# Step two of a graph layer: the first pair's order, and who makes the lists of tied values

## The reference

```python
for n in range(2):                                  # the steps
    logits = (Xa @ W1.T @ W2.T) @ (Xa @ W3.T).T     # 3327 x 3327
    probs = softmax(logits)
    # nucleus: of each row the largest values are kept, until those
    # ahead of a value sum to 0.9; the order among equals is argsort's
    sp = take_along_axis(probs, argsort(-probs)); cs = cumsum(sp)
    mask = (cs - sp < 0.9) put back in place
    A = probs * mask / sum(probs * mask)
    Xf = R @ Xf                                     # R: adj + I, rows normed
    Xa = A @ Xa
    Z = Z + Xf @ U1[n].T + Xa @ U2[n].T
x = layernorm(X + Z)
```

## Time and profile before

| | us |
|---|---|
| median of three runs | 2841.34 |
| the profiled execution, by its own time | 2843.26 |
| span of the profiled execution | 2841.4 |
| TensorE (PE) busy | 2368.2 (83%) |
| VectorE busy | 2228.3 (78%) |
| ScalarE busy | 1071.9 (38%) |
| GpSimd busy | 97.5 (3%) |

### The profile page before, as it was taken

The page is one execution under the profiler, slowest core; times in us unless marked ns, Lnnn a source line. Parts: engine busy times, 40 slices in busy tenths (PEclk is TensorE's granted clock), DMA queues, the critical chain, the costliest instruction groups (busy, mean ns, idle before and its releaser), DMA issues. The chain is left out here.

```text
span 2841.4 us, 53527 instructions
## 1 busy us (share of the span) xinstructions
PE 2368.2 (83%) x17759; PEld 1995.4 (70%) x17759; DVE 2228.3 (78%) x6754; ACT 1071.9 (38%) x1785; POOL 97.5 (3%) x236
## 2 busy tenths in 40 slices
PE   5898998755888888887887728996999999999985
PEld 1566666444777676666676627895899999999952
DVE  3777778358887889887888967784999999999946
ACT  4566666422333334333343131002443434434323
POOL 0000000100000000000000010000000000000000
PEclk9999999977889998999998967998999999999997
DMA  3000000020222221222221232563233434343320
GB/s 125 2 1 1 1 1 2 1 73 25 98 98 98 97 98 50 98 83 75 77 107 50 97 126 100 214 216 124 98 130 116 137 107 145 103 144 109 112 86 25
DMA packets 57109, 245.02 MB, mean 86 GB/s; under 512 B 6705, under 2 KB 18352, under 8 KB 43120
## 3 DMA queue, kind: packets, MB, share of 16 engines
q1 hardware_dynamic: 56816, 241.94, 24.2%
HBM read 235.10 MB, written 6.82 MB: 85 GB/s over the span
## 5 line engine op out<-in xcount | busy, mean ns | idle before, releaser
L1906 PE MATMUL a_acc<-H,pT 128*128 128x128 f32 x4056 | 548.0, 277 | 11.3 <-ACT a_rows L1938 3.7
L1906 PEld LDWEIGHTS a_acc<-H,pT 128*128 128x128 f32 x4056 | 495.4, 192 | 28.3 <-DVE pT L2040 19.8
L913 PE MATMUL small<-XR,wT 128*128 128x128 f32 x2756 | 376.4, 282 | 30.4 <-ACT wT L1109 29.6
L71 DVE MAX8 cand<-e 128x8 f32<-128x64 f32 (+3 forms) x1898 | 302.5, 239 | 123.4 <-issue 123.4
L797 PE MATMUL lg<-kT,qs 128*128 128x512 f32 (+1 forms) x742 | 351.9, 614 | 46.0 <-ACT e L1053 36.1
L913 PEld LDWEIGHTS small<-XR,wT 128*128 128x128 f32 x2756 | 342.1, 196 | 46.6 <-ACT wT L1109 46.6
L2040 DVE TENSOR_TENSOR pT<-a_tr,a_adjT 128x512 f32<-128x512 f32 (+1 forms) x546 | 316.6, 645 | 22.6 <-PE a_tr L1865 19.2
L817 PE MATMUL accR<-XR,adj 128*128 128x129 f32 x2704 | 329.4, 284 | 0.0
L817 PEld LDWEIGHTS accR<-XR,adj 128*128 128x128 f32 x2704 | 326.3, 202 | 0.0
L1865 PE MATMUL a_tr<-ident,prob 128*128 128x128 f32 x2028 | 311.7, 274 | 10.9 <-ACTq L1932 10.9
L1109 ACT ACTIVATE wT<-tr 128x512 f32<-128x512 f32 (+1 forms) x371 | 206.1, 566 | 278.6 <-PE tr L903 276.7
(11 more groups left out here) (329 smaller groups left out, 2457.4 us busy)
## 6 DMA issues: line engine op xcount, KB each, us to landing
adj<-in_adjT SPq DMA_DIRECT2D x52, 1664.0 KB, 7.2
g_adj<-in_adjT SPq DMA_DIRECT2D x26, 1664.0 KB, 6.9
a_adj<-in_adj SPq DMA_DIRECT2D x26, 1664.0 KB, 6.9
a_adjT<-in_adjT SPq DMA_DIRECT2D x156, 256.0 KB, 3.9
a_adjT<-in_adjT SPq DMA_DIRECT2D x26, 128.0 KB, 4.2
XT<-in_x_t SPq DMA_DIRECT2D x1, 1664.0 KB, 13.4
hT_scratch<-hT SPq DMA_DIRECT2D x1, 1664.0 KB, 12.4
nsT_scratch<-nsT SPq DMA_DIRECT2D x1, 1664.0 KB, 6.2
```

Source lines behind the costliest of these rows:

```text
L71: eng.max(cand[:, n, :], src[:, n * seg:min((n + 1) * seg, width)])
L913: mm = eng.matmul(accA[:, :], wT[(k * NC + c - 1) % 2][:, o:o + P], xa[:, j, 0:P], start=(j == 0), stop=(j == T - 1))
L1906: mm = eng.matmul(acc[:, :], pT[g % RING][:, (j % 4) * P:(j % 4 + 1) * P], H[:, j, :], start=(j == 0), stop=(j == T - 1))
```

## The change

In step two alone:

1. GpSimd makes the grid ahead of the queries of pairs 0 and 1. TensorE makes its part of the grid after the logits of pair 0, ahead of those of pair 1. ScalarE copies the grid ahead of pair 0's exponentials, and copies unit 1's rows ahead of pair 1's exponentials.
2. A new function `find_marks` on GpSimd makes the drops and hits of both tiles of a pair, into buffers that now have room for two tiles. It waits for the pair's flags and for the selections of the pair before, and is done one pair ahead, between the scaling and the adding of rows. VectorE waits for the new semaphore `marks_ready` ahead of its selections and finds nothing more itself, but for the last batch. The instruction that moves `left` on is a function of its own, `pass_ties`, which runs only where more than 24 ties are to be marked.
3. In the first hop GpSimd scales the rows of both units of a pair before it adds either.

```diff
@@ Search
-        self.hits, self.drops = sb("hits", [P, TIES]), sb("drops", [P, 8])
+        self.hits, self.drops = sb("hits", [P, 2, TIES]), sb("drops", [P, 2, 8])
...
     def find_ties(self, eng, k):
+        hits = self.hits[:, k, :]
+        eng.tensor_scalar(hits, self.index[:, :], self.one("cut", k), None, ALU.mult)
+        eng.drain()
+        eng.tensor_scalar(hits, hits, self.one("left", k), self.one("cut_kept", k), ALU.is_lt, ALU.mult)
+        eng.drain()
+
+    def pass_ties(self, eng, k):
         eng.scalar_tensor_tensor(self.one("left", k), self.one("cut", k), -float(TIES), self.one("left", k),
                                  ALU.mult, ALU.add)
+        eng.drain()
...
-    def select(self, eng, k, e_pad, kind, flag, regs, both_ways):
+    def select(self, eng, k, e_pad, kind, flag, regs, both_ways, found=False):
...
         def divide():
-            if both_ways:
-                self.find_drops(eng, k)
-            self.find_ties(eng, k)
-            self.mark_ties(eng, 0, e_pad)
+            if not found:
+                if both_ways:
+                    self.find_drops(eng, k)
+                self.find_ties(eng, k)
+            self.mark_ties(eng, k, 0, e_pad)
...
@@ gpsimd
+                    def find_marks(p):
+                        eng.wait_ge(flags_ready, turn_of(step, p) + 1)
+                        eng.wait_ge(w_ready, seq(step, p, 0))
+                        eng.tensor_tensor(pool_gate[:, :], find.one("cut", 0), find.one("cut", 1), ALU.add)
+                        for k in range(2):
+                            find.find_drops(eng, k)
+                            find.find_ties(eng, k)
+                        eng.drain()
+                        eng.sem_inc(marks_ready, 1)
...
                         else:
+                            if hop == 0:
+                                for u, s in units_of(p, hop):
+                                    scale_rows(u, s)
+                            find_marks(p + 1)
                             for u, s in units_of(p, hop):
-                                if hop == 0:
-                                    scale_rows(u, s)
                                 add_rows(u, hop)
                             give_attended(p)
...
+                    if step == 1:
+                        make_grid()
                     for p in range(2):
                         give_q(p, 0)
                         give_q(p, 1)
-                    if step == 1:
-                        make_grid()
                     if step == 0:
                         over_pairs(eng, pair, tail=3)
                     else:
+                        find_marks(0)
                         over_pairs_with_rows(eng, pair_with_rows)
@@ tensor
                     for p in range(2):
                         logits(p, 0)
                         logits(p, 1)
+                        if step == 1 and p == 0:
+                            make_grid()
...
-                        make_grid()
                         for u, s in units_of(0, 0):
                             rows(u, 0)
@@ scalar
                     for k in range(2):
                         copy_logits(0, 0, k)
+                    if step == 1:
+                        copy_grid()
                     for k in range(2):
                         exps(0, 0, k)
...
-                        copy_grid()
                         copy_rows(0, 0, 0)
+                        copy_rows(1, 1, 0)
                         exps_of(1, 1)
-                        copy_rows(1, 1, 0)
@@ vector
-                        find.select(eng, k, e[b][k][:, :], kinds[k], flag, regs, step == 1)
+                        find.select(eng, k, e[b][k][:, :], kinds[k], flag, regs, step == 1,
+                                    found=step == 1 and not at(p, PAIRS))
...
                         assign_slots(p)
+                        eng.wait_ge(marks_ready, p + 1)
+                        eng.memset(gate[:, :], 0.0)
                         select(p, b, 0)
                         select(p, b, 1)
```

More of the change, by code:

```diff
@@ L416, in find_ties, with mark_ties, drop_ties @@
     def find_ties(self, eng, k):
-        eng.tensor_scalar(self.hits[:, :], self.index[:, :], self.one("cut", k), None, ALU.mult)
+        hits = self.hits[:, k, :]
+        eng.tensor_scalar(hits, self.index[:, :], self.one("cut", k), None, ALU.mult)
         eng.drain()
-        eng.tensor_scalar(self.hits[:, :], self.hits[:, :], self.one("left", k), self.one("cut_kept", k),
-                          ALU.is_lt, ALU.mult)
+        eng.tensor_scalar(hits, hits, self.one("left", k), self.one("cut_kept", k), ALU.is_lt, ALU.mult)
         eng.drain()
+    def pass_ties(self, eng, k):
         eng.scalar_tensor_tensor(self.one("left", k), self.one("cut", k), -float(TIES), self.one("left", k),
                                  ALU.mult, ALU.add)
+        eng.drain()
     def find_drops(self, eng, k):
-        eng.tensor_scalar(self.drops[:, :], self.index[:, 0:8], self.one("cut", k), None, ALU.mult)
+        drops = self.drops[:, k, :]
+        eng.tensor_scalar(drops, self.index[:, 0:8], self.one("cut", k), None, ALU.mult)
         eng.drain()
[L430 to L435, removed]
+        eng.tensor_scalar(drops, drops, self.one("over", k), self.one("cut_dropped", k), ALU.is_le, ALU.mult)
+    def mark_ties(self, eng, k, n, src):
+        eng.match_replace(out=self.work[:, :], in_to_replace=self.hits[:, k, 8 * n:8 * n + 8], in_values=src,
                           imm_value=BIG_E)
-    def drop_ties(self, eng):
-        eng.match_replace(out=self.work[:, ::-1], in_to_replace=self.drops[:, :], in_values=self.work[:, ::-1],
+    def drop_ties(self, eng, k):
+        eng.match_replace(out=self.work[:, ::-1], in_to_replace=self.drops[:, k, :], in_values=self.work[:, ::-1],
                           imm_value=-1.0)
@@ L459, in more_ties @@
             for n in range(TIES // 8):
-                self.mark_ties(eng, n, self.work[:, :])
+                self.mark_ties(eng, k, n, self.work[:, :])
                 eng.drain()
+            self.pass_ties(eng, k)
             eng.tensor_scalar(self.one("r_up", k), self.one("left", k), 0.0, 4.0, ALU.is_gt, ALU.mult)
@@ L481, in divide @@
                 self.find_ties(eng, k)
-                self.mark_ties(eng, 0, e_pad)
+                self.mark_ties(eng, k, 0, e_pad)
             eng.drain()
             if both_ways:
-                self.drop_ties(eng)
+                self.drop_ties(eng, k)
             with eng.If(eng.snap(flag) > 1):
                 eng.drain()
-                self.mark_ties(eng, 1, self.work[:, :])
+                self.mark_ties(eng, k, 1, self.work[:, :])
                 with eng.If(eng.snap(flag) > 2):
                     eng.drain()
-                    self.mark_ties(eng, 2, self.work[:, :])
+                    self.mark_ties(eng, k, 2, self.work[:, :])
                     eng.drain()
+                    self.pass_ties(eng, k)
                     while_over(eng, flag, 3, self.width // TIES, more_ties)
@@ L547, in layer0 @@
         qs = [sb(f"qs{i}", [P, P]) for i in range(2)]
-        gate = sb("gate", [P, 1])
+        gate, pool_gate = sb("gate", [P, 1]), sb("pool_gate", [P, 1])
         inv_sums = sb("inv_sums", [P, T])
@@ L589, in layer0 @@
         grid_ready, grid_made, grid_copied = sem("l0_grid_ready"), sem("l0_grid_made"), sem("l0_grid_copied")
+        marks_ready = sem("l0_marks_ready")
         slots_ready, taken_ready = sem("l0_slots_ready"), sem("l0_taken_ready")
```

## The result

The changed kernel took 2792.97 us, the median of four runs from 2790.32 to 2795.52, beside 2840.43 for the kernel before (four runs). The ratio is 0.9826 with a 95% interval of 0.9804 to 0.9848, so 49.4 us less (43 to 56). The profiled execution took 2795.35 us, with a span of 2793.6, TensorE busy 2358.4 (84%), VectorE 2201.9 (79%), ScalarE 1071.5 (38%), GpSimd 140.9 (5%).

What follows compares the result with a forecast made beforehand. VectorE's chain was taken to bound step two: 23.9 (first pair) + 33.6 (lists) - 1.0 - 1.2 = 55.3 us off the profiled 2843.26 gives 2788.0, median 2786.0. Range 2770 to 2806.

Steps and rivals of the forecast that it cites:

- VectorE is the chain in step two, and waits for other engines at two places only: Step two: time off VectorE comes off the span; it waits only for the grid, 19.0 us, and TensorE's flags, 16.1.
- Part one, 23.9: Start of step two: grid and unit one's rows copied earlier bring VectorE's first slot instruction to 618.6, gaining 23.9 us.
- The shift by 2.2: Start of step two: GpSimd's grid ahead of the first queries makes all up to the search come 2.2 us later.
- Part two, 33.6 for 13 pairs: Selections: drops and hits leave VectorE, 33.0 + 1.5 us, less 0.9 for a wait and memset per pair: 33.6 us.
- The lists are hidden: GpSimd's lists take about 4 us per pair under 19.9 us of cover; the last pair may lose 0 to 2.
- Scaling in the search, 1.0 lost: VectorE's search, six pairs: the second unit's scaling beside it costs 0.2 us each, 1.0 us in all.
- The lock rule: VectorE's search: shared port charges it GpSimd's 1.28 us in six pairs, 7.7 us, sum 48.6; rival at 2793, chance 0.05.
- TensorE's slack, 1.2 lost: TensorE's wait for flags at pair 12: its own way is 211.3 us, VectorE's would be 210.1, so 1.2 us is lost.
- all slack: TensorE's 15.0 us of waits for GpSimd's scaling go away, but all of it is slack today.
- the gaps stay: VectorE's 25 gaps ending in "issue", 63.5 us: the number of jumps stays; a change over 16 us refutes the prediction.
- the first rival: VectorE's gaps are dealt anew by the changed code, 16 us either way: 2770 or 2802; chance 0.12 better, 0.12 worse.
- the second, TensorE as the limit: In the pairs TensorE becomes the limit and half of the lists' gain is eaten: 2803 us; chance 0.08.

Runs made afterwards that it cites:

- e10: The changed kernel itself, unchanged, measured and profiled again: 2790.36 us, ratio 0.982.
- e1: The kernel before with only the first pair's new order (grid early, unit one's rows copied ahead of pair one's exponentials): 2816.33 us, ratio 0.9906.
- e2: The changed kernel with the old order at the start of step two, so only the lists on GpSimd: 2809.52 us, ratio 0.9888.
- e4: The changed kernel with GpSimd making each pair's lists twice, same values: 2795.91 us, ratio 0.9841.
- e7: The changed kernel with GpSimd making each pair's lists six times: 2908.37 us, ratio 1.0235.
- e11: The changed kernel with a pair's second unit scaled behind the first unit's adding, as before the change: 2798.84 us, ratio 0.9852.
- e8: The kernel before, unchanged, profiled once more: 2841.59 us in one execution.
- e6: The changed kernel with GpSimd making the grid between pair 0's and pair 1's queries: 2784.52 us, ratio 0.9795.
- e12: The changed kernel with the grid between pair 0's and pair 1's queries, measured a second time: 2785.5 us, ratio 0.9789.
- e3: The changed kernel with eight more drains in each selection's jumped-over block for a finer search: 2803.71 us, ratio 0.9863.
- e5: The changed kernel with each selection's jumped-over block for a finer search written once, not twice: 2786.7 us, ratio 0.981.

## Why the prediction was right, and where it missed

The direction, the range and both mechanisms held: 55.3 us forecast, 49.4 measured (52.1 in e10), with an interval that just reaches the forecast. Point by point:

- *VectorE is the chain in step two, and waits for other engines at two places only*: right for the most part, wrong in one. What e1 and e2 took off VectorE came off the span nearly whole, and TensorE's waits for it stayed at 46.1 us. But VectorE waits at a third place, ahead of the tops, for logits: 29.7 us in nine gaps before. The prediction took these for gaps behind a branch or a loop's return, in which nothing was awaited.
- *Part one, 23.9*: 24.1 in the profile, 24.5 alone in e1. The shift by 2.2, the search at 576.4 (576.75), the DMA-gated unit at 604.6 (604.34), its end and the slots at 618.6 (618.45) came as worked out.
- *Part two, 33.6 for 13 pairs*: without gaps, 33 us in 12 pairs and 2.8 in the rest (820.2 to 787.1). That is right or a little low, but "without gaps" leaves out that the gaps grew.
- *The lists are hidden*: right, 4.07 us against 4, and 0.54 lost in pair 12. e4 shows the cover, e7 its end.
- *Scaling in the search, 1.0 lost*: about 2 us. The searches of pairs 1 to 6 take 146.1 us in sum after and 146.2 before, but that compares two things at once: those of pairs 2 and 4, which have no scaling beside them in either kernel, are 0.4 us shorter after. e11, with the changed kernel's code on VectorE, gives the price: 2.1 us, in the searches of pairs 1, 3, 5 and 6. In pairs 2 and 4 both units are scaled before the search begins. GpSimd pays too: its multiply has a mean of 436 ns in place of 400, the copy 399 in place of 368. The lock rule of the Trainium skill (SBUF — State Buffer, section on two separate sides), by which the prediction came to 7.7 us, is not borne out as a price for VectorE: some 11 us more of GpSimd's work lie in these searches than in e11. That the two engines meet, the trace agrees, by these times. The prediction's 1.28 us for a unit also left out its two multiplies of 0.40 each.
- *TensorE's slack, 1.2 lost*: not at the flags; VectorE waits 1.35 us for pair 12's flags, 1.70 before. It shows ahead of the tops instead, where the waits for logits went from 29.7 us to 33.8. And the sentence that TensorE's 15.0 us for scaling were "all slack" failed: it holds for the kernel before and no longer for the changed one, as e11 shows with 4 to 8.5 us. The sum over the stage (82 us) hid that in four pairs of the first hop TensorE is within 3 us of VectorE.
- *The step that failed in the sum is that the gaps stay.* They grew by 9.3 us, which is the 6 us that are missing and more; it is the first rival, at some three fifths of its price, and in part the second, TensorE as the limit. By place: waits for logits +4.1, gaps behind a branch +2.9, and 2.2 from two gaps that passed the bound of 1 us by 0.1. Means of the three profiles with the lists on VectorE (before, e8, e1) and of six with the lists on GpSimd (after, e10, e2, e4, e6, e12) say the same: waits for logits 28.0 and 32.6, gaps behind a branch 34.3 and 38.6. The growth is in pairs 8 to 11: 16.6 to 21.3 us in the three, 28.9 to 31.4 in the six, and never under 26.4 in the five other runs with the lists on GpSimd. In pairs 0 to 7 the two kinds don't differ (41.0 to 45.5, 40.6 to 44.7 us). The way says it without any count of gaps: the lists are worth 2.6 us a pair, 20.8 in pairs 0 to 7 and 10.4 in pairs 8 to 11, and 21.0 and 2.7 were gained.
- *Why*, for the logits: the chain from a pair's selection over TensorE's products and logits and ScalarE's copies to a later pair's tops holds no list, so it got no shorter, while VectorE comes to its tops sooner. At the longest wait of each kernel that is 9.61 us in place of 6.75. This is read from the order of the work in the traces; no run tests it. For the gaps behind a branch: ahead of the drops they grew in pairs 8 to 11 from 2.6 us (2.1 in e8, 3.3 in e1) to between 8.9 and 10.3 in the six; there the jump of each pair's second selection took 2.9 to 4.8 us in the first profile of before and 5.5 to 6.0 in that of after. So the growth goes with the change and not with chance. e3 shows that code that isn't run moves such gaps. Whether here it is VectorE's shorter code or something else in the change stays open, and so does by what rule a jump takes 0.5, about 3 or about 6 us.
- The Trainium skill (Runtime: NRT & Kernel Launch, Instruction fetch mechanics) has a branch out of the fetched pages stall. The trace agrees as far as it goes: the gaps ahead of the drops and at the loop's return stand right behind a compare-and-branch, and in e5, with less to jump over, some of these jumps take 0.5 us. No run here shows what was fetched when.

So the number came nearer than its terms did, and that part is luck: 33.6 less 2.2 of losses was forecast for part two, 35.9 came without the gaps, and this unforeseen surplus hides nearly half of the 9.3 us by which the gaps grew.

## What to carry to other kernels

Follow a wait at a stage's start through all the engines: here two copies in the wrong place on ScalarE cost about three quarters of what the small instructions of 13 pairs did. Before you call a gap one in which nothing was awaited, look at the instruction that starts in the same moment and at what ended just before: here nearly half of such idle time was a wait for another engine's copies. Small instructions on a bound engine are worth their start-to-start distance, not their busy time, and an idle engine does them free if the data is ready a stage earlier; look then at what is queued behind them there. Where the bound engine's code has large blocks that are jumped over, as here, leave some 10 us of room in the forecast, and compare versions of an edit at that size by repeated runs only.

## What the runs showed that I had not expected

- The largest gaps marked "issue" were waits for logits.
- Eight unexecuted instructions in each selection made the kernel 10.7 us slower (e3).
- GpSimd takes 314 to 461 ns for a multiply or compare of 128 x 8 or 128 x 24 with per-partition scalars, where VectorE takes 231 to 297; a width of 24 in place of 8 adds 0.04 to 0.05 us (0.31 and 0.36, 0.41 and 0.46).
- VectorE's MAX8 ran at its pace (6.67 to 6.69 us for a tile's 52, in all profiles) with 8 us of GpSimd work beside it (e4), and with 24.5 (e7).
- The second layer, the same code in all, took 1169.7 to 1180.1 us in 14 profiles, so one profile can't settle a question of 5 us.
